# Unused bytes between the operands of the matmuls: another distance modulo 512 bytes for each kind of product, in a group norm and attention block in split float32

## What is computed

```python
    xn = group_norm(x, gamma, beta)
    xf = xn.reshape(B, N, C)
    q = xf @ wq + bq
    k = xf @ wk + bk
    v = xf @ wv + bv
    scores = jnp.einsum('bnc,bmc->bnm', q, k) * C ** (-0.5)
    attn = jax.nn.softmax(scores, axis=-1)
    out = jnp.einsum('bnm,bmc->bnc', attn, v)
    out = out @ wp + bp
    return out.reshape(B, H, W, C) + residual
```

## The kernel before

| kind | line | held | moving | matmuls in an image | in all 16 |
|---|---|---|---|---|---|
| t chunk | 788-790 | `a_hi`, `a_lo` | `xn_hi`, `xn_lo` | 96 | 1,536 |
| v tile | 788-790 | `xn_hi`, `xn_lo` | `m_hi`, `m_lo` | 96 | 1,536 |
| score tile | 788-790 | `xn_hi`, `xn_lo` | `t_hi`, `t_lo` | 192 | 3,072 |
| output tile | 871-873 | `pt_hi`, `pt_lo` | `v_hi`, `v_lo` | 192 | 3,072 |

## Time and profile before

### The profile page before, as it was taken

How to read it: one execution, slowest core, us unless ns; L and a number is a source line. 1 busy time by engine, 2 the same in 40 slices (tenths; PEclk the granted TensorE clock), 3 DMA queues, 4 the chain that set the end, 5 groups by cost and what they waited for, 6 DMA issues and landing times.

```text
span 2180.9 us, 28171 instructions
## 1 busy us (share of the span) xinstructions
PE 2153.6 (99%) x9425; PEld 1762.9 (81%) x9425; DVE 1434.9 (66%) x2280; ACT 672.7 (31%) x1113; POOL 829.6 (38%) x487
## 2 busy tenths in 40 slices
PE   6999999999999999999999999999999999999998
PEld 5788888888888888888888888888888888888886
DVE  6775675856668475774756758576684757748454
ACT  3241332414233132331413324142331323314231
POOL 3344343433433335332443434334333343324433
PEclk9999999999999999999999999999999999999999
DMA  7003021030302103021030210303021030210201
GB/s 169 20 15 102 1 73 43 29 86 0 96 19 58 58 5 101 10 63 53 14 101 0 72 43 29 86 0 96 19 58 58 5 101 10 63 53 10 68 0 59
DMA packets 109259, 106.03 MB, mean 49 GB/s; under 512 B 8492, under 2 KB 74032, under 8 KB 109232
## 3 DMA queue, kind: packets, MB, share of 16 engines
q1 hardware_dynamic: 109184, 105.68, 17.3%
q10 hardware_dynamic: 48, 0.01, 0.0%
HBM read 72.10 MB, written 33.55 MB: 48 GB/s over the span
## 4 chain that ended last, share of the span: by engine, by line
PE 94%; POOL 2%; issue 2%; SPq 1%; DMA 1%; ACT 0%; DVE 0%; POOLq 0%; ACTq 0%; DVEq 0%
PE psum L788 21%; PE psum L790 21%; PE psum L789 21%; PE psum L873 10%; PE psum L871 10%; PE psum L872 10%; SPq L234 1%; DMA w_p<-in_L_conv_wp_dram 1%; POOL total_part L344 0%; POOL bias_part L370 0%; POOL x_res L322 0%; SPq L249 0%; ACT score L456 0%; POOL out_bias L374 0%; PE psum L834 0%
## 5 line engine op out<-in xcount | busy, mean ns | idle before, releaser
L788 PE MATMUL psum<-t_hi,xn_hi 128*128 128x512 f32 x1024 | 406.4, 397 | 1.3 <-DVE v_lo L524 1.3
L790 PE MATMUL psum<-t_hi,xn_lo 128*128 128x512 f32 x1024 | 405.0, 396 | 0.0
L789 PE MATMUL psum<-t_lo,xn_hi 128*128 128x512 f32 x1024 | 405.0, 395 | 0.0
L871 PE MATMUL psum<-v_hi,pt_hi 128*128 128x512 f32 x1024 | 399.1, 390 | 4.5 <-DVE pt_lo L524 4.5
L873 PE MATMUL psum<-v_hi,pt_lo 128*128 128x512 f32 x1024 | 398.6, 389 | 0.0
L872 PE MATMUL psum<-v_lo,pt_hi 128*128 128x512 f32 x1024 | 398.6, 389 | 0.0
L322 POOL TENSOR_TENSOR x_res<-x_res,out_bias 128x512 f32<-128x512 f32 (+1 forms) x144 | 179.7, 1259 | 437.1 <-issue 233.8
L616 DVE TENSOR_TENSOR top_part<-top_part,score 128x512 f32<-128x512 f32 x192 | 169.3, 882 | 254.6 <-ACT score L451 253.1
L451 ACT ACTIVATE score<-psum 128x512 f32<-128x512 f32 x256 | 151.3, 599 | 481.3 <-PE psum L790 481.3
L344 POOL TENSOR_TENSOR total_part<-total_part,score 128x512 f32<-128x512 f32 x192 | 279.4, 1455 | 46.2 <-ACT score L456 31.5
L456 ACT ACTIVATE score<-score 128x512 f32<-128x512 f32 x256 | 157.5, 633 | 293.7 <-DVE score L632 293.7
(11 more groups left out here) (101 smaller groups left out, 2995.0 us busy)
## 6 DMA issues: line engine op xcount, KB each, us to landing
x_res<-in_x_dram SPq DMA_DIRECT2D x128, 256.0 KB, 2.9
out_dram<-x_res SPq DMA_DIRECT2D x128, 256.0 KB, 2.1
x_blk<-in_x_dram SPq DMA_DIRECT2D x240, 128.0 KB, 2.9
score<-in_x_dram SPq DMA_DIRECT2D x16, 128.0 KB, 7.8
w_q<-in_L_conv_wq_dram SPq DMA_DIRECT2D x4, 256.0 KB, 4.8
w_k<-in_L_conv_wk_dram SPq DMA_DIRECT2D x4, 256.0 KB, 8.0
w_v<-in_L_conv_wv_dram SPq DMA_DIRECT2D x4, 256.0 KB, 8.4
w_p<-in_L_conv_wp_dram SPq DMA_DIRECT2D x1, 1024.0 KB, 11.4
```

The costliest lines, as they stand in the source:

```text
L788: nc.tensor.matmul(dst, s_hi_, m_hi_, start=n == 0, stop=False)
L789: nc.tensor.matmul(dst, s_hi_, m_lo_, start=False, stop=False)
L790: last = nc.tensor.matmul(dst, s_lo_, m_hi_, start=False, stop=n == len(pairs) - 1)
L871: nc.tensor.matmul(dst, pt_hi[:, m, queries], v_hi[:, m, :], start=m == 0, stop=False)
```

## The change

Unused tensors of 16, 16 and 40 numbers per partition (64, 64 and 160 bytes) are allocated ahead of `a_hi`, of `m_hi` and of `t_hi`. `v_hi` and `v_lo` get 8 more numbers (32 bytes) per partition, of which 4 lie ahead of the data and 4 behind it. Nothing is ever written to or read from these bytes. No instruction is added, removed or moved.

```diff
         xn_hi = sb("xn_hi", [P, KC, N], F32R)
         xn_lo = sb("xn_lo", [P, KC, N], F32R)
+        sb("a_offset", [P, 16])
         a_hi = sb("a_hi", [P, KC, C], F32R)
         a_lo = sb("a_lo", [P, KC, C], F32R)
+        sb("m_offset", [P, 16])
         m_hi = sb("m_hi", [P, KC, C], F32R)
         m_lo = sb("m_lo", [P, KC, C], F32R)
...
+        sb("t_offset", [P, 40])
         t_hi = sb("t_hi", [P, KC, BANK], F32R)
         t_lo = sb("t_lo", [P, KC, BANK], F32R)
-        v_hi = sb("v_hi", [P, NT, C], F32R)
-        v_lo = sb("v_lo", [P, NT, C], F32R)
+        v_hi, v_lo = (sb(n, [P, NT * C + 8], F32R)[:, 4:NT * C + 4].rearrange("p (m c) -> p m c", m=NT)
+                      for n in ("v_hi", "v_lo"))
         pt_hi = sb("pt_hi", [P, NT, BANK], F32R)
         pt_lo = sb("pt_lo", [P, NT, BANK], F32R)
```

## The result

The changed kernel is slower: 2203.15 us, median of 4 launches (2202.38 to 2204.32), against 2180.93 us, the median of 4 launches of the kernel before (2180.29 to 2183.83). The ratio is 1.0098, 95% interval 1.0083 to 1.0113. The time lies inside the range of the prediction, but the prediction had the sign wrong. The profiled execution took 2202.97 us with a span of 2201.2, 20.3 us more than before.

What follows compares the result with a forecast made beforehand. TensorE's matmul intervals were taken as the bound: 41 us off t, v and attention plus 31 off scores, 2 us given back, took 2182.6 to 2112.6, or 2111 us after adjusting to the median; range 2075 to 2226.

Steps and rivals of the forecast that it cites:

- What bounds the kernel: TensorE bounds it end to end; matmul starts 226.7 ns apart, 233.3 in scores, against a floor of 213.3; 144 us lost.
- The change part by part: New moving-minus-held distances: t chunks -64, v tiles +128, scores 256, attention -48 and -16; no instruction, wait or transfer added.
- Pricing VectorE at nothing: VectorE's instructions on moved tensors lie beside TensorE; `pt_lo` has 3.9 us of cover, so price 0.
- Between ends I take half of today's loss as gone in each kind: All four kinds: 6.7 ns less per matmul in t, v and attention, 10.0 in scores; together 72 us off.
- The step down to 528 cycles (220.0 ns): Matmul intervals of 544 and 560 cycles read as steps of 16, making 528 the next level for t, v and attention.
- The ceiling of 235 ns: Upper bound for matmul intervals at the new distances, taken from the longer intervals right after TensorE switches kinds.
- Rival 1: Zero is the good distance, every other costs a crossing per load: t, v, attention +41 us, scores unchanged; 2221; chance 0.35.
- Its point of decision: In the TensorE matmuls: the slower case decides as soon as more than half end above 230 ns.
- Rival 2: Only distance modulo 64 bytes counts: t and v stay, scores -20.5 us, attention taken as 0; 2160; chance 0.12.
- Rival 3: Nothing changes: distance is idle in TensorE's matmuls, or kinds gain and lose alike; 2180; chance 0.09.
- The range: Whole kernel, eight in ten: 2075 to 2226, drawn to reach the slow case and its spread.
- the chance of 0.56 for faster: Whole kernel: the chance of a faster result, the forecast's 0.44 together with the modulo-64 case's 0.12.

Runs made afterwards that it cites:

- run 1: Kernel of before with 32 unused bytes ahead of `t_hi` alone, all four kinds of product at distance 0; 2160.87 us, ratio 0.9903.
- run 2: Kernel of before with 288 unused bytes ahead of `t_hi` alone: scores at distance 256, the other kinds at 0; 2161.19 us.
- run 4: Kernel of before with unused bytes that put all four kinds of product at distance 256; 2161.8 us.
- Run 3: Kernel of before with `a`, held in the t chunks, moved by 64 bytes and everything behind it kept at its old residue; 2190.74 us.
- run 8: Kernel of before, the middle matmul of each three in score and output tiles holding 64 columns in place of 128; 2187.12 us.
- run 14: Kernel of before, score and output matmuls save the first and last of each group holding 64 of 128 columns; 2187.08 us.
- run 15: Kernel of before, score and output matmuls save the first and last of each group holding 32 of 128 columns; 2198.21 us.
- run 10: Kernel of before with other unused bytes: distances modulo 256 of t chunks 96, v tiles 80, scores 48, output tiles 112; 2202.09 us.
- run 11: Kernel of before with other unused bytes: distances modulo 256 of t chunks 144, v tiles 176, scores 208, output tiles 240; 2204.5 us.
- run 13: Kernel of before with other unused bytes: scores at distance +240, output tiles at -16, t chunks and v tiles at 0; 2211.0 us.
- run 12: Kernel of before with other unused bytes: distances modulo 256 of t chunks 4, v tiles -48, scores -16, output tiles 8; 2220.74 us.

## Why the prediction was wrong

**What bounds the kernel** stood. TensorE's intervals carry the whole difference, waits none of it: those for `pt_lo`, `xn_lo` and `v_lo` are 3.3 + 2.6 + 1.7 = 7.6 us, before 8.5.

**The change part by part.** The instruction counts stayed and the five distances are what I worked out. That distance has a price was right as well, and run 1 shows it where the argument had taken it from, in the scores. Pricing VectorE at nothing held: `pt_lo` holds TensorE up by 3.3 us in all, before 4.5.

**The step that failed** is "Between ends I take half of today's loss as gone in each kind". It has the wrong sign for three kinds: t lost 6.6 ns where I wrote a gain of 6.7, v lost 5.8, the output tiles 7.6. What the runs show in the place of that step is that 0 and 256 are the good distances: there all four kinds run at 226.7 ns (runs 1, 2 and 4), and each of the other four distances of the change costs something. In the scores the sign was right and the size 6.6 in place of 10.0. I had one steady non-zero distance, and it was the dear one; three kinds at 0 were the cheap ones. The step down to 528 cycles (220.0 ns) was arithmetic on two values with no row behind it. No stage of the 17 kernels settles there; the least is 226.7 ns, and no twelve intervals in a row within a stage average less than 226.5. The ceiling of 235 ns was a little low, with 235.5 in 15 stages.

**Rival 1** had the sign right in three kinds and nearly the size, with 6.7 ns against 5.8 to 7.6 measured. Its point of decision was passed too: two thirds of the matmuls stand above 230 ns. The single intervals that it cited the earlier trace rows say nothing, since the one at distance 0 was 0.24 us as well. The stretches behind them do, and the prediction read them the other way: it held that a stretch behind a switch is slow at distance 0 too, but run 1 has none. The rival missed the scores: it held every other distance to be dear, and 256 isn't. With that its mechanism, one crossing per load at every distance but 0, is refuted as it stands. Its 2221 less the 20 us of the scores is 2201, 2 us from the measurement, with v lower and the output tiles higher than it had them.

**Rival 2** said that 256 is the old 0, and scores fall by 20.5 us: so they did. But its 64 bytes are refuted by t at -64 (233.3 ns), v at 128 (232.5) and scores at 64 (228.9).

**Rival 3** falls with run 1, in which 32 unused bytes take 22 us off. The Trainium skill (TensorE: Matmul & The Clock Gate, What happens when you issue a matmul) says that loading the next weights takes no bandwidth from the running matmul. Run 3 moved only the address that the load reads, and the matmul beside it went from 226.7 to 233.4 ns. So for these matmuls the running one is not left alone by the load beside it, and the measurement decides; whether it is bandwidth that it loses isn't shown. The 215.8 ns of the section Back-to-back issue gap of that page, which it gives for the isolated matmul, aren't reached in any stage either.

**The range** held the time only because it was drawn wide enough for rival 1; the chance of 0.56 for faster was not earned by the rows.

**What stays open** is how the load and the stream hinder each other. It is shown that the interval depends on the address of the load (run 3), that it changes when fewer columns are held (runs 8, 14, 15), that at one distance it can take several values and change behind an interruption (runs 10, 11, 13), and that at 0 and 256 with full loads the stages settle at 226.7 ns. A picture that gives those numbers I don't have: a loss in proportion to the load is refuted, and the single crossing of rival 1 gives no reason for 228.9 ns at 64 and 12, nor for two states at 112. Whether the remaining 13.4 ns at distance 0 come from the load was not tried with loads taken away, since every matmul here brings its own.

## What to carry to other kernels

Where TensorE is the bound and weight loads alternate with streams of 512 float32r columns, work out the addresses modulo 256 of each product's two operands, and try them at the same residue: 32 unused bytes ahead of one tensor were worth 1% here, and a handful of small tensors allocated in between had cost it. Other types and other lengths of stream were not run. Read the cost as the distance between starts, stage by stage, and not from the duration of a row. When the trace holds one good and one bad value of a quantity, moving every user off the good one is a bet against the only evidence there is.

## What the runs showed of the hardware

- Intervals over distances modulo 256 (means of stages): 0: 226.7 ns in all kinds. 64: 228.9. 80, 16, 128: 231.0, 231.7, 232.3 to 232.5. 32, 96, 144, 176, 192, 224: 233.3. 160: 234.3. 4 and 8 bytes: 233.1 and 233.3; 12: 228.9; -4: 232.3. Two or more values: 48 (230.0 in 15 stages of 47, 233.3 in the others), 208 (means of 231.2 in v tiles and 234.5 in scores), 112 (226.7 in 15 output stages, 233.3 in 16), 240 (226.7 in 30 output stages of run 11; 233.3 and 236.7 in the scores of runs 12 and 13). No distance had less than the 226.7 ns of 0.
- Behind two products of four columns a stage went from 233.3 to 236.6 ns for its remaining 71 matmuls (run 13, distance 240), and behind waits and a fall of the clock from 226.6 to 236.6 (run 11, distance 240). At distances 0 and 256 the interval was back at 226.7 ns after ten matmuls at the most behind a stage of another kind, pauses aside; in run 1, with 0 everywhere, it was there from the first.
- Fewer held columns made matmuls at distance 0 slower, though their loads were shorter: 226.7, 229.8 and 231.4 ns with 128, 64 and 32 columns held, beside loads of 188, 134 and 109 ns.
